# First attention of a two-layer kernel: some VectorE work handed to ScalarE, and one bias matmul per pair of tiles

## What is computed

```python
xn = (x - mean(x)) / sqrt(var(x) + 1e-5)
q, k, v = xn @ Wq.T + bq, xn @ Wk.T + bk, xn @ Wv.T + bv     # 16, 8, 8 heads of 16
q = q * cos + rotate_half(q) * sin                           # the same for k
def feats(y):                                                # R is 8 x 16
    y = y / maximum(norm(y), 1e-6)
    p = y @ R.T
    return concatenate([sin(p), cos(p)]) / 4                 # 16 features
kv  = einsum('bhsf,bhsd->bsfd', feats(k), v)                 # k and v repeated to 16 heads
out = einsum('bhsf,bsfd->bhsd', feats(q), kv)                # per token
```

## Time and profile before

| | us |
|---|---|
| median of three runs | 1841.6 |
| the profiled execution | 1837.6 |
| its span | 1835.8 |
| busy in the span: TensorE (matmul) | 1597.9 |
| VectorE | 1380.6 |
| ScalarE | 1031.0 |
| GpSimd | 667.8 |
| first attention, from start to the next stage's first loads | 0 to 323.3 |

### The profile page before, as it was taken

The page is one execution under the profiler, slowest core; times in us unless marked ns, Lnnn a source line. Parts: engine busy times, 40 slices in busy tenths (PEclk is TensorE's granted clock), DMA queues, the critical chain, the costliest instruction groups (busy, mean ns, idle before and its releaser), DMA issues. The chain is left out here.

```text
span 1835.8 us, 34559 instructions
## 1 busy us (share of the span) xinstructions
PE 1597.9 (87%) x9650; PEld 1238.0 (67%) x9650; DVE 1380.6 (75%) x3710; ACT 1031.0 (56%) x2457; POOL 667.8 (36%) x842
## 2 busy tenths in 40 slices
PE   6996886689954786999999999996899999988896
PEld 5885765579953563554555555544799999977775
DVE  7899998266657877999888888833666666667777
ACT  2664654256656660566676767674556666543443
POOL 2655687400027623111237667620000000056662
PEclk9998999789986995999999999998999999999998
DMA  9333456644435885432435545413864444355552
GB/s 343 130 87 85 106 146 167 205 137 133 133 116 168 290 306 149 99 74 61 106 97 156 160 142 171 128 61 122 274 201 133 133 134 133 117 166 164 169 165 75
DMA packets 279591, 272.72 MB, mean 149 GB/s; under 512 B 121769, under 2 KB 248426, under 8 KB 277356
## 3 DMA queue, kind: packets, MB, share of 16 engines
q1 hardware_dynamic: 255672, 215.41, 39.8%
q0 software_dynamic: 18432, 50.36, 9.0%
q10 hardware_dynamic: 5332, 4.96, 0.8%
HBM read 136.84 MB, written 133.69 MB: 147 GB/s over the span
## 5 line engine op out<-in xcount | busy, mean ns | idle before, releaser
L1890 ACT ACTIVATE ca_PT<-ca_psS 128x512 f32<-128x512 f32 (+3 forms) x768 | 336.3, 494 | 202.9 <-PE ca_psS L1927 197.8
L1430 POOL DMA_INDIRECT g_y<-ys_scratch,pos x128 | 125.0, 977 | 428.2 <-POOLq L73 357.0
L1806 DVE CUSTOM_DVE_ANT_0 ca_masked_row<-ca_psM,mask_row 128x384 f32<-128x384 f32 (+3 forms) x512 | 224.3, 486 | 44.4 <-PE ca_psM L1910 42.4
L1927 PE MATMUL ca_psS<-ca_QS,ca_KS 128*128 128x512 f32 (+1 forms) x480 | 174.7, 367 | 1.4 <-ACT ca_PT L1890 1.4
L1810 DVE TENSOR_REDUCE ca_part<-ca_psM 128x1 f32<-128x512 f32 x256 | 163.4, 685 | 16.1 <-PE ca_psM L1910 14.7
L1939 PE MATMUL ca_psO<-ca_PT,ca_VA 128*17 128x512 f32 (+3 forms) x1536 | 161.0, 491 | 6.0 <-ACT ca_OT L1882 5.9
L1910 PE MATMUL ca_psM<-ca_KS,ca_QS 126*128 126x512 f32 (+2 forms) x480 | 159.0, 379 | 6.5 <-DVE ca_part L1806 4.2
L797 PE MATMUL fa_psO<-fa_weighed,ident 128*128 128x256 f32 x512 | 127.9, 407 | 38.1 <-DVE fa_weighed L585 38.1
L1927 PEld LDWEIGHTS ca_psS<-ca_QS,ca_KS 128*128 128x128 f32 x480 | 90.2, 189 | 86.8 <-ACT ca_PT L1890 58.1
L391 POOL DMA_INDIRECT xs_scratch<-x_sb,pos x128 | 124.6, 973 | 55.9 <-ACT ca_PT L1890 34.1
L797 PEld LDWEIGHTS fa_psO<-fa_weighed,ident 128*128 128x128 f32 x512 | 101.7, 204 | 59.0 <-DVE fa_weighed L585 44.6
(11 more groups left out here) (271 smaller groups left out, 4638.5 us busy)
## 6 DMA issues: line engine op xcount, KB each, us to landing
xs_scratch<-fa_blank SPq DMA_DIRECT2D x32, 640.0 KB, 4.9
x_sb<-xs_scratch SPq DMA_DIRECT2D x143, 128.0 KB, 2.1
ys_scratch<-x_sb SPq DMA_DIRECT2D x143, 128.0 KB, 1.7
xs_scratch<-fa_blank SPq DMA_DIRECT2D x32, 384.0 KB, 6.4
spare<-qk_scratch SPq DMA_DIRECT2D x24, 512.0 KB
ca_QS<-qk_scratch SPq DMA_DIRECT2D x20, 512.0 KB, 6.1
ca_KS<-qk_scratch SPq DMA_DIRECT2D x20, 512.0 KB, 7.6
x_sb<-in_ffn SPq DMA_DIRECT2D x16, 608.0 KB, 4.5
```

The source lines that it names most:

```text
L1430: pool.indirect_dma_start(y[:, t % R, k, :], None, y_dram, bass.IndirectOffsetOnAxis(pos[:, t, k:k + 1], 0)).then_inc(got[t % R], 16)
L1806: ins = dve.tensor_tensor_reduce(masked_row[:, (n * NU + u) % BANKS, h * w:(h + 1) * w], bank[:, h * w:(h + 1) * w], mask_row[:, CHUNK - w ...
L1890: act.activation(PT[:, s % PTS, h, off:CHUNK], psS[(GH * s + h) % BANKS][:, off:CHUNK], ACT.Exp)\
L1927: pe.matmul(psS[tile % BANKS][:, off:CHUNK], KS[slot][:, h, kt * P:(kt + 1) * P], QS[slot][:, h, c * CHUNK + off:(c + 1) * CHUNK], start=T ...
```

## The change

- **Normalised rows go to ScalarE.** `inverse_root` also makes shift = -mean x rstd on VectorE, and `normalise` becomes an Identity activation with scale and bias per token on ScalarE. Step 1 normalises two pairs ahead of the first high half, later steps one pair each. `root` moves to the end of ScalarE's step (a new hook `after` of `in_steps`).
- **The root's table is loaded first.** A square root of two numbers (`warm`) stands ahead of the copy of the weights.
- **Rounding goes to ScalarE.** `whole_turns` is a Copy with bias ROUND, between the copy and the square of the next tile's q and k, and `fraction` subtracts ROUND and the turns in one instruction with two tensor inputs, as before. Its sign is turned for q and k alike, so the squares of the sines are the same.
- **Centring becomes a ninth summand.** `apart` has a ninth column that holds -4, written once. `centre` goes, and `sine_sums` reads nine columns.
- **One bias matmul for two tiles**, over 272 columns, ahead of a pair's value matmuls.
- **Weights are split ahead of the bias**, the first low half stands between the bias instructions, and TensorE waits for the bias only before the first bias matmul.
- In VectorE's table the square sums move ahead of the fraction. `rot_b` has one buffer in place of two.

```diff
-        qk, rot_a, rot_b, rot, sq, rotT = (sb(x, [P, 2, NQK]) for x in ("qk", "rot_a", "rot_b", "rot", "sq", "rotT"))
+        qk, rot_a, rot, sq, rotT = (sb(x, [P, 2, NQK]) for x in ("qk", "rot_a", "rot", "sq", "rotT"))
+        rot_b = sb("rot_b", [P, NQK])
+        shift, warm = sb("shift", [P, TILES]), sb("warm", [2, 1])
...
-        apart = sb("apart", [P, 2, HEADS, KV_HEADS, RF])
+        apart = sb("apart", [P, 2, HEADS, KV_HEADS, RF + 1])
...
-                dve.reciprocal(some, some).then_inc(rstd_done, 1)
-
-            def normalise(q):
-                dve.wait_ge(rstd_done, q * PAIR // GROUP + 1)
-                for t in range(PAIR * q, PAIR * (q + 1)):
-                    dve.tensor_scalar(rows[:, t, :], x_sb[:, t, :], mean_rstd[:, t, 0:1], mean_rstd[:, t, 1:2], ALU.subtract, ALU.mult)\
-                       .then_inc(xn_done, 1)
+                dve.reciprocal(some, some).then_inc(rstd_part, 1)
+                dve.wait_ge(rstd_part, g + 1)
+                dve.scalar_tensor_tensor(shift[:, GROUP * g:GROUP * (g + 1)], mean_rstd[:, GROUP * g:GROUP * (g + 1), 0], -1.0, some,
+                                         ALU.mult, ALU.mult).then_inc(rstd_done, 1)
...
-            def whole_turns(t, i, b):
-                dve.wait_ge(turns_part, t * 2 + 1)
-                dve.tensor_scalar(whole[:, i % 2, :, :], turns[:, i % 2, :, :], ROUND, ROUND, ALU.add, ALU.subtract)\
-                   .then_inc(turns_part, 1)
-
             def fraction(t, i, b):
-                dve.wait_ge(turns_part, t * 2 + 2)
+                dve.wait_ge(whole_done, t + 1)
                 f = turns[:, i % 2, :, :]
-                dve.tensor_tensor(f, f, whole[:, i % 2, :, :], ALU.subtract).then_inc(turns_done, 1)
+                dve.scalar_tensor_tensor(f, whole[:, i % 2, :, :], ROUND, f, ALU.subtract, ALU.subtract).then_inc(turns_done, 1)
...
-                dve.tensor_tensor(apart[:, i % 2, :, :, :], q4, k4, ALU.subtract).then_inc(apart_done, 1)
+                dve.tensor_tensor(apart[:, i % 2, :, :, 0:RF], q4, k4, ALU.subtract).then_inc(apart_done, 1)
...
-            def centre(t, i, b):
+            def weigh(t, i, b):
...
+            def split_weights_and_bias():
+                dve.wait_ge(whi_done, 1)
+                dve.tensor_tensor(w_all[1], w_raw[:], w_all[0].bitcast(F32), ALU.subtract).then_inc(wlo_done, 1)
+                dve.wait_ge(ident_in, 16)
+                dve.wait_ge(bias_in, 16)
+                s = Steps(dve, bias_part)
+                s.link(dve.tensor_copy(b_hi[:, :], bias[:, :]))
+                s.link(dve.tensor_tensor(b_lo[:, :], bias[:, :], b_hi[:, :].bitcast(F32), ALU.subtract))
+                low_half(0)
+                s.link(dve.tensor_scalar(b_lo[:, :], b_lo[:, :], ident[0:2, 1:2], None, ALU.mult))
+                s.link(dve.scalar_tensor_tensor(b_two[:, :], b_hi[:, :].bitcast(F32), ident[0:2, 0:1], b_lo[:, :], ALU.mult, ALU.add))
...
-            in_steps(dve, (5, bounded_norm), (11, sine_sums), (5, inverse_norm), (8, in_turns), (11, centre), (8, whole_turns), (11, weigh),
-                     (8, fraction), (3, square_norm), (9, differences), first=BESIDE, beside=beside)
+            dve.wait_ge(ones_done, 3)
+            in_steps(dve, (5, bounded_norm), (11, sine_sums), (5, inverse_norm), (8, in_turns), (11, weigh), (3, square_norm),
+                     (8, fraction), (9, differences), first=BESIDE, beside=beside)
...
+            def normalise(q):
+                act.wait_ge(rstd_done, q * PAIR // GROUP + 1)
+                for t in range(PAIR * q, PAIR * (q + 1)):
+                    act.activation(rows[:, t, :], x_sb[:, t, :], ACT.Identity, scale=mean_rstd[:, t, 1:2], bias=shift[:, t:t + 1])\
+                       .then_inc(xn_done, 1)
...
-            def take_qkv(t, i, b):
+            def take_qk(t, i, b):
                 act.wait_ge(qk_done, t + 1)
                 if late(t, 2):
                     act.wait_ge(rot_done, t - 1)
                 act.activation(qk[:, i % 2, :], psQ[:, 0:NQK], ACT.Copy).then_inc(qk_out, 1)
...
+            def whole_turns(t, i, b):
+                act.wait_ge(turns_part, t + 1)
+                act.activation(whole[:, i % 2, :, :], turns[:, i % 2, :, :], ACT.Copy, bias=ROUND).then_inc(whole_done, 1)
+
+            def square_qk(t, i, b):
+                act.wait_ge(qk_done, t + 1)
                 if late(t, 2):
                     act.wait_ge(n2_done, t - 1)
                 act.activation(sq[:, i % 2, :], psQ[:, 0:NQK], ACT.Square).then_inc(sq_done, 1)
...
+                if n == 1:
+                    normalise(0)
+                    normalise(1)
                 if 0 <= n - 1 < PAIRS:
                     high_half(n - 1)
+                if 2 <= n < PAIRS:
+                    normalise(n)
...
+            def after(n):
+                if n < QUADS:
+                    root(n)
...
+            act.wait_ge(ones_done, 1)
+            act.activation(warm[:, :], ones[:, 0:1].bitcast(F32), ACT.Sqrt)
             act.wait_ge(w_in, 16)
             act.activation(w_all[0], w_raw[:], ACT.Copy).then_inc(whi_done, 1)
-            in_steps(act, (2, take_qkv), (10, sines), (3, keep_rotT), (13, take_out), (10, squares), (4, keep_p),
-                     (4, norm), first=BESIDE, beside=beside)
+            in_steps(act, (2, take_qk), (8, whole_turns), (2, square_qk), (10, sines), (3, keep_rotT), (13, take_out), (10, squares),
+                     (4, keep_p), (4, norm), first=BESIDE, beside=beside, after=after)
...
+                if t >= 1:
+                    pool.wait_ge(rot_done, t)
...
+            pool.memset(apart[:, :, :, :, RF:RF + 1], -RF / 2.0).then_inc(ones_done, 1)
...
+                if t == 0:
+                    pe.wait_ge(bias_part, 4)
...
+                pe.matmul(psV[:, 0:PAIR * NVE].rearrange("p (t n) -> p t n", n=NVE), ones[:],
+                          b_two[:, NQK:W0].unsqueeze(1).broadcast_to([2, PAIR, NVE]), start=True, stop=False, skip_group_check=True)
                 for j, t in enumerate(range(PAIR * q, PAIR * (q + 1))):
-                    out = psV[:, j * NVE:(j + 1) * NVE]
-                    three_passes(pe, out, lambda k: x_hi(t, k), lambda k: x_lo(t, k), lambda k: w_all[0][:, k, NQK:W0],
-                                 lambda k: w_all[1][:, k, NQK:W0], KT, last=False, check=True)
-                    ins = pe.matmul(out, ones[:], b_two[:, NQK:W0], start=False, stop=True, skip_group_check=True)
+                    ins = three_passes(pe, psV[:, j * NVE:(j + 1) * NVE], lambda k: x_hi(t, k), lambda k: x_lo(t, k),
+                                       lambda k: w_all[0][:, k, NQK:W0], lambda k: w_all[1][:, k, NQK:W0], KT, first=False, check=True)
```

41 lines of the change are left out of this document (12 added, 29 removed).

## The result

The changed kernel takes 1830.06 us, the median of eight runs (1826.8 to 1835.7); the kernel before, over its eight, takes 1840.05. The ratio is 0.9949, with a 95% interval of 0.9931 to 0.9966: 9.4 us faster, between 6 and 13. Run again twice beside the kernel before, the change gave 0.9947 and 0.9955. The forecast was a gain of 18.8 us. The direction was right and the size half.

The account below looks back on a forecast made before the run. TensorE was taken to set the pace to 130 us, then VectorE. Gains of 7.5 + 4.9 + 0 + 5.9 + 0.5 = 18.8 us from 1837.6 gave 1818.8, forecast as 1820 us, range 1809 to 1831.

Parts of the forecast that it names:

- Part 1: Start of the first attention: the first projection begins near 12.0 us instead of 19.56; gain 7.5 us, bounds 6.0 to 8.3.
- The clock: TensorE's rise from 1.2 to 2.4 GHz, near 37 us before, assumed to follow the same work and move with the start.
- rival B: TensorE's clock does not move with the work: still at 37 us, 4 us lost; a projection earlier, 4 gained; chance 0.12.
- Part 2: TensorE's stretch to 130 us: the joint bias matmul saves 0.29 us for most of 16 pairs, 4.9 us in all.
- Part 3: VectorE's stretch, 16 steps (18 to 33): centring and rounding leave VectorE; 0.37 us per step, 5.9 us in all.
- Rival E: ScalarE's ring, from VectorE's turns through rounding, square and sines to VectorE's sums, makes the kernel slower; chance 0.03.
- rival A: The hold-up between VectorE and GpSimd keeps the gain: 0.17 us for each of 16 steps, 2.7 us, 1823; chance 0.15.
- Part 4: Last nine steps of the first attention: 0.17 us each, reduced for a sine table load and GpSimd's scatters; gain 0.5 us.

## Why the prediction was right in direction and wrong in size

**Part 1, the start, 7.5: right, with some luck in the sum.** The projection started at 12.06 against 12.0; alone the start was worth 8.6 us (5.5 to 11.8). A normalisation takes 0.52 and not 0.38, and the weights came 0.6 earlier than in the profile before. With the weights as late as there (7.03, in a profile with the square first) the projection starts at 12.60, a gain of 7.0.

**The clock: wrong in 11 of 15 profiles, in the kernel's favour.** "I assume that the rise comes after the same amount of work." In the change the value matmuls at 22.2 us already take 0.28, after 10 us of projections instead of 17.7. In four other profiles with this start the rise comes as assumed: with the square first a projection matmul at 27.92 still takes 0.52, a value matmul at 31.10 takes 0.28. The early rise gave 15.8 us at tile 0 where 12.4 was the sum of parts 1 and 2, and it is not the kernel's own: see the last section. It is the better half of rival B, "a projection earlier, 4 gained".

**Part 2, the joint bias, 4.9: right where TensorE sets the pace.** 0.29 per pair was forecast, the steps shortened by 0.33 to 0.35. Taking it out of the kernel with the square first cost 3 to 7 us. Alone on the kernel before it showed 0.4 (-1.8 to 2.8). Parts 1 and 2 with the ninth summand, and with the square sums ahead of the fraction, make the kernel with the rounding on VectorE: 12.3 us measured (9.2 to 15.5) against 7.5 + 4.9 = 12.4.

**Part 3, 5.9: this step failed.** The prediction read "I take 0.37, nearer the low end" for each of 16 steps. The undisturbed 0.17 was right (5.30 to 5.14), though only for both small operations together. Beside GpSimd a step did not fall from 7.4 to 7.0, it rose to 7.60 to 7.77. Against the kernel with the rounding on VectorE the rounding's move took some 3 us (0.9949, 0.9947 and 0.9955 against 0.9933), where part 3 had a gain; that it took time is within the intervals, but it did not bring 5.9, which would have put the change at 0.990. Two things stood in place of the relief.

The first is the ring. Rival E had the right place, the rounding ahead of the square, but followed it only through the sines to VectorE's sums, and found room: that held (VectorE waited there 1.1 us in all). It did not follow what stands behind the rounding in ScalarE's step: the square, and then every copy that GpSimd and TensorE wait for. So VectorE's turns release the copy of q and k, and through rotation, transposes, group sums and random projection the roots that VectorE needs first in a later step. VectorE waited there 8.3 to 13.2 us, in the kernel before not at all. The order of two instructions in it cost 5 to 6 us, and that is shown; by which of its branches is not: no time is lost where TensorE waits at psQ. Nor does the order matter everywhere: on the kernel before, with the centring on VectorE, both orders took 1846.3. It is not rival E's outcome either: the kernel was still faster.

The second is rival A. With the square first the step is 7.17 to 7.22 where the forecast had 6.9 to 7.0. That is 0.17 to 0.22 less than before, which is A's price for a step, the undisturbed 0.17, and nothing for the hold-ups. Even that is not the rounding's: with it on VectorE the step is 7.13, and VectorE is busy 7.07 us of it against 7.06. The Trainium skill ("SBUF — State Buffer", SBUF: two separate sides) has VectorE's and GpSimd's port pair as an exclusive lock. The trace agrees that the two hold each other up: taking three of GpSimd's four operations out shortened the mean weighing from 2.72 to 2.29 us and VectorE's step by 0.85 us, to 6.37, while VectorE's own list of work stayed the same.

**Part 4, 0.5: wrong in sign.** In the last nine steps the change went from 14.4 us ahead to 13.2; 0.8 came back in the five last, undisturbed ones (12.4 to 13.2), as 0.16 each has it, and 2.0 went in the four ahead of them.

Sum as it stands: start, bias and ninth summand 12.3, rounding -3, together 9.3, where 9.4 was measured. It closes because the -3 is itself the difference of two measured kernels; it is no second measurement. Alone on the kernel before, start, bias, ninth summand and rounding come to 8.6, 0.4, -0.7 and -7.7, together 0.6, so the parts do not add, and what each is worth depends on the others. One error was lucky: some 4 us more by the clock at tile 0 of the profiled start stand against the loss in part 3.

A version beats both kernels: the change with the square of q and k ahead of the rounding, 1821.9, 1823.8 and 1823.6 us, ratios 0.991 to 0.9933. With it the change comes to some 14 us of the 18.8 forecast.

## What to carry to other kernels

When an operation that waits for another engine is put into an in-order engine's step, list every instruction queued behind it and ask who waits for each; then put it behind those that don't need it, and compare the order on the chip, since a wait that shows in a table need not cost anything. Price small operations that stand beside each other as a group: each may lie in the other's waiting time, so that one alone is worth nothing and both together are worth something. Where two engines hold each other up, relief of one may be no gain until the other's work shrinks too.

## What the runs showed of the hardware that was not expected

The moment at which TensorE's clock rises is not fixed by the work. Up to the third copy of q and k the 15 profiles with the new start have the same matmuls on TensorE (two of them with a bias matmul per tile), but in 11 these run at 2.4 GHz by then, in the other four not. Two rows of the same instruction, a value matmul, of the change and of the kernel with the square first:

```profile
22.22 0.28 PE L121 MATMUL fa_psV<-wqkvr_lo,spare 128*128 128x136 f32 x1
```

```profile
23.43 0.41 PE L121 MATMUL fa_psV<-wqkvr_lo,spare 128*128 128x136 f32 x1
```

There, in the second, the third copy of q and k comes 7.5 us after the second, where it is 4.55 in the change. Tile 0 was weighed at 65.05, and in the two repeats of that same kernel at 61.1 and 61.0: 4 us from nothing in the code. The kernel with rounding on VectorE has the late rise in its profile too (7.52), the three profiles of the change all the early one. So a difference of 4 us between two single profiles of a start that TensorE bounds says nothing. The Trainium skill ("TensorE: Matmul & The Clock Gate", The HAM clock gate) says that the number of slow matmuls at the start varies from run to run; the runs agree.

A root after a copy needed no pause beyond its table load: in the rows at 208 us the copy ends at 208.41, the load starts at 208.43 and takes 1.28, and the root runs at 209.72. The Trainium skill ("ScalarE: Activation LUTs", What ACT_TABLE_LOAD costs) puts a drain of 1.38 us on top; in these rows there is none, nor at 8.14 in the kernel before, where the load follows a copy and the root starts at 9.43.
